# Turning the normalised rows by blocks on VectorE and placing them by transfers, places sent tile by tile, and one shared tile for the ends of W1 and W2

## The reference

```python
x = x + xattn(layernorm(x), ctx, ctx, mask)         # 16 heads, softmax(q k^T / 4) v, then w_o
y = layernorm(x);  idx = top_k(y @ w_router, 128)   # ffn layer, per batch
h = rmsnorm(y[idx], g1); attn = causal_attention(h @ W_qkv.T) @ W_out.T
h2 = rmsnorm(y[idx] + attn, g2)
ff = silu(h2 @ W1.T) * (h2 @ W2.T) @ W3.T           # inner width 682 = 5 x 128 + 42
out = x + y with rows idx of y replaced by y[idx] + attn + ff
```

## Time and profile before

| | us |
|---|---|
| median of 3 runs (lowest, highest) | 889.56 (888.82, 891.79) |
| the profiled execution | 880.62 |
| its span | 878.9 |
| PE busy | 852.3 (97%) |
| ACT busy | 570.7 (65%) |
| DVE busy | 312.4 (36%) |
| POOL busy | 122.7 (14%) |

### The profile page before, as it was taken

One profiled execution on the slowest core, in us unless ns is written; L12 is line 12 of the kernel. 1 busy time (PEld: TensorE's weight loads), 2 busy tenths in 40 slices (PEclk: granted clock), 3 DMA queues, 4 the chain that ended last, 5 costly groups with the idle time before them and its releaser, 6 DMA issues. The chain is left out here.

```text
span 878.9 us, 28281 instructions
## 1 busy us (share of the span) xinstructions
PE 852.3 (97%) x11797; PEld 297.4 (34%) x11802; DVE 312.4 (36%) x915; ACT 570.7 (65%) x648; POOL 122.7 (14%) x174
## 2 busy tenths in 40 slices
PE   7999999999999999999999999999999999999875
PEld 2322232334323433334323333233323342234343
DVE  3122245421552326421453216522274213322442
ACT  3567667676677767676677766777676766776310
POOL 4000102110120101111121101201021101200111
PEclk9999999999999999999999999999999999999999
DMA  5060101120011200211011200112002100010000
GB/s 186 14 234 3 64 17 33 54 76 11 3 37 50 80 8 27 61 32 50 8 39 50 80 8 2 37 50 80 7 5 60 32 3 7 14 49 3 7 25 11
DMA packets 27579, 35.58 MB, mean 40 GB/s; under 512 B 2083, under 2 KB 24142, under 8 KB 27448
## 3 DMA queue, kind: packets, MB, share of 16 engines
q1 hardware_dynamic: 24952, 31.73, 11.3%
q0 software_dynamic: 2496, 1.98, 1.4%
HBM read 27.53 MB, written 8.93 MB: 41 GB/s over the span
## 5 line engine op out<-in xcount | busy, mean ns | idle before, releaser
L524 ACT ACTIVATE probs<-pair_bank 128x1024 f32<-128x1024 f32 x512 | 496.4, 1021 | 222.9 <-ACTq L523 221.7
L494 PE MATMUL pair_bank<-q_sb,k_sb 32*64 32x512 f32 x4096 | 291.2, 612 | 0.4 <-PEq L492 0.3
L513 PE MATMUL o_bank<-probs,va 128*32 128x512 f32 x2048 | 274.7, 604 | 3.0 <-issue 1.5
L513 PEld LDWEIGHTS o_bank<-probs,va 128*32 128x32 f32 x2048 | 41.7, 108 | 208.2 <-issue 113.8
L494 PEld LDWEIGHTS pair_bank<-q_sb,k_sb 32*64 32x64 f32 x4096 | 62.3, 129 | 134.8 <-issue 133.5
L271 PE MATMUL m_bank<-wv_sb,ctx_in 128*32 128x256 f32 x1024 | 62.2, 380 | 0.0
L271 PE MATMUL m_bank<-ctx_in,wk_sb 128*32 128x512 f32 x480 | 61.0, 592 | 0.0
L649 DVE TENSOR_SCALAR va<-m_bank,valid 128x256 f32<-128x256 f32 x64 | 28.1, 479 | 82.8 <-DVEq L646 82.7
L605 DVE STREAM_TRANSPOSE o_blk<-o_bank 128x512 f32<-128x512 f32 x32 | 22.9, 717 | 96.4 <-DVEq L604 96.4
L271 PEld LDWEIGHTS m_bank<-wv_sb,ctx_in 128*32 128x32 f32 x1024 | 33.5, 110 | 35.9 <-issue 21.3
L271 PEld LDWEIGHTS m_bank<-hid_t,w 128*32 128x32 f32 x1392 | 39.4, 110 | 17.2 <-issue 16.3
(11 more groups left out here) (175 smaller groups left out, 627.3 us busy)
## 6 DMA issues: line engine op xcount, KB each, us to landing
ctx_in<-in_ctxT SPq DMA_DIRECT2D x7, 1024.0 KB, 4.9
x_in<-in_x SPq DMA_DIRECT2D x8, 512.0 KB, 3.9
x<-in_x SPq DMA_DIRECT2D x8, 512.0 KB, 4.3
mask_in<-in_mask SPq DMA_DIRECT2D x8, 512.0 KB, 3.9
out_dram<-base SPq DMA_DIRECT2D x8, 512.0 KB, 5.6
ctx_in<-in_ctxT SPq DMA_DIRECT2D x2, 512.0 KB, 6.9
mask_row<-in_mask SPq DMA_DIRECT2D x8, 128.0 KB, 3.9
x_tok<-in_order SPq DMA_DIRECT2D x7, 128.5 KB, 2.0
```

The source lines that it names most:

```text
L494: last = nc.tensor.matmul(pair_bank[pairs[r // 2]][j:j + 64, r % 2], key_tile(b, s, r)[:, j:j + 64], query_tile(b, s, r), start=True, stop ...
L513: last = nc.tensor.matmul(o_bank[32 * r:32 * r + 32], va[b % 2][:, t, HV * h:HV * h + 32], probs[s % 2][:, r], start=(t == 0), stop=(t == ...
L524: nc.scalar.activation(probs[s % 2][:, 2 * e:2 * e + 2, :], pair_bank[p][:], ACT.Exp, scale=HD ** -0.5).then_inc(s_free[p], 1)
```

## The change

Six things are done.

1. From batch 1 on, TensorE no longer turns the normalised rows. VectorE writes them so that 32x32 blocks lie where a block transpose needs them (stage `blocks`) and turns them by two transposes of 128x512 (stage `turn`). Four transfers place the blocks into a DRAM tensor `turned`, and a fifth loads `xn_t` (`put_blocks`). `Q0`, `Q1` become `R0`, `R1` and wait for that load. Batch 0 keeps the old way.
2. For that `x` is loaded with another mapping of rows to partitions, in four transfers (`load_x_for_blocks`).
3. In the loop the stages `stats`, `blocks` and `turn` stand at the end of VectorE's order for batch b+2, around `down`. GpSimd's `var` moves with them. Batch 0 runs them twice: for batch 1, and at its end for batch 2.
4. ScalarE loses the two copies into `xn_t`, TensorE's steps 7 and 8 (in batch 0, 18 and 21) have no third part.
5. Each tile's place is written right behind its own ranking, with a `drain` ahead of it.
6. The last 42 rows of W2 lie in the free columns of W1's sixth tile. So `w1` has two tiles and not three, and VectorE has two small instructions more (`w_rest`, and the product for those 42 rows).

```diff
-           ("P", "K11:0", 4, False), ("P", "K11:1", 5, False), ("F", "spread", 6, False), ("P", "xT0", 7, False), ("P", "xT1", 8, False),
-           ("P", "Q0:0", 9, False), ("P", "Q0:1", 10, False), ("P", "V1", 11, False), ("P", "Q1:0", 12, False), ("P", "Q1:1", 13, False),
+           ("P", "K11:0", 4, False), ("P", "K11:1", 5, False), ("F", "spread", 6, False),
+           ("P", "R0:0", 9, False), ("P", "R0:1", 10, False), ("P", "V1", 11, False), ("P", "R1:0", 12, False), ("P", "R1:1", 13, False),
...
-POOL_ORDER = [("F", "var"), ("P", "var"), ("F", "scatter"), ("F", "rms0"), ("F", "causal"), ("F", "rms1"), ("P", "differ"), ("F", "add")]
+POOL_ORDER = [("F", "var"), ("F", "scatter"), ("F", "rms0"), ("F", "causal"), ("F", "rms1"), ("P", "differ"), ("X", "var"), ("F", "add")]
+POOL_ORDER_0 = [("P", "var"), ("P", "differ"), ("X", "var")]
...
+        def load_x_for_blocks(sp, b):
+            sp.wait_ge(x_free, 1)
+            sp.sem_inc(x_free, -1)
+            for a in range(QT):
+                sp.dma_start(x_in[32 * a:32 * a + 32], io["x"][b, a * P:(a + 1) * P].rearrange("(t i) d -> i t d", i=32)
+                             ).then_inc(x_ready, 16)
+        def put_blocks(sp):
+            sp.wait_ge(blocks_ready, 1)
+            sp.sem_inc(blocks_ready, -1)
+            for a in range(QT):
+                sp.dma_start(turned[:, a * P:(a + 1) * P].rearrange("(c j) k -> j c k", j=32),
+                             blocks_t[32 * a:32 * a + 32].rearrange("j (c k) -> j c k", k=P)).then_inc(blocks_stored, 16)
+            sp.wait_ge(blocks_stored, 16 * QT)
+            sp.sem_inc(blocks_stored, -16 * QT)
+            sp.wait_ge(x_t_free, 1)
+            sp.sem_inc(x_t_free, -1)
+            sp.dma_start(xn_t[:], turned.rearrange("(c p) s -> p c s", p=P)).then_inc(x_t_ready, 16)
...
-                for f in range(3):
+                for f in range(2 if stage == "w1" else 3):
...
+            elif stage == "blocks":
+                dve.wait_ge(rstd_ready, 1)
+                dve.sem_inc(rstd_ready, -1)
+                by_block = xn[:].rearrange("p t d -> p (t d)").rearrange("p (c t j) -> p c t j", t=QT, j=32)
+                for t in range(QT):
+                    nc.vector.tensor_scalar(by_block[:, :, t], x_in[:, t].rearrange("p (c j) -> p c j", j=32), mv[:, t, 0:1],
+                                            rstd[:, t:t + 1], ALU.subtract, ALU.mult)
+                dve.drain().then_inc(x_free, 1)
+            elif stage == "turn":
+                flat = xn[:].rearrange("p t d -> p (t d)")
+                for half in (slice(0, S), slice(S, 2 * S)):
+                    nc.vector.transpose(blocks_t[:, half], flat[:, half])
+                dve.drain().then_inc(blocks_ready, 1)
...
-                if t > 0:
+                if note is put:
+                    dve.drain()
+                    put(t)
+                elif t > 0:
                     note(t - 1)
...
+                if r == 1:
+                    last = nc.vector.tensor_scalar(w_rest[:], bank[i][W2_REST:W2_REST + REST, 2 * P:3 * P], 0.5, None, ALU.mult)
+                last.then_inc(bank_free[i], 1)
...
+                if r == 1:
+                    nc.vector.tensor_tensor(gate[0:REST, FT - 1], w_rest[:], silu2[r][0:REST, 2 * P:3 * P], ALU.mult)
...
                 for b in range(B):
-                    if b + 2 < B:
-                        load_x(sp, b + 2)
+                    if b == 0:
+                        put_blocks(sp)
+                        load_x_for_blocks(sp, 2)
                     if b > 0:
                         load_selected(sp, b - 1)
...
                         load_ctx(sp, b + 2)
+                        put_blocks(sp)
+                    if b + 3 < B:
+                        load_x_for_blocks(sp, b + 3)
```

More of the change, by code:

```diff
@@ L28 @@
 FT = 6
+REST = DFF - (FT - 1) * P
+W2_REST = 64
 BIG = 2.0 ** 30
@@ L188, in program @@
         silu2 = [sb(f"silu2{r}", [P, 3 * P]) for r in range(2)]
+        w_rest = sb("w_rest", [REST, P])
         gate = sb("gate", [P, FT, P])
```

65 lines of the change are left out of this document (41 added, 24 removed), and 13 rows, old and new, of tables (DVE_ORDER, PE_SLOT_0).

## The result

The changed kernel takes 877.92 us (median of 4 runs, 876.13 to 878.86), the kernel before, run beside it, 889.19 us (888.12 to 891.79): a ratio of 0.9867, 95% interval 0.984 to 0.9894, or 11.3 us less. The forecast was 882.5 us and 7.1 us less. The profiled execution after took 877.64 us, which is also the middle of its plain runs; that of before (880.62) is not. By the profiles the two kernels differ by 3.0 us, by the plain runs by 11.3. The reason for this gap turned out to be the cause of the error too.

The account below looks back on a forecast made before the run. TensorE, busy 97% of the span, was taken as the bound. 5.0 + 0.2 + 3.1 - 1.2 = 7.1 us gained gave 873.5 us profiled and 882.5 us as the median of runs, range 877.5 to 888.

Parts of the forecast that it names:

- steps 7 and 8, batches 1 to 6: TensorE steps losing their transposes: the pair takes 4.43 us instead of 5.26, 0.83 per batch, 5.0 us gained.
- steps 18 to 22 of batch 0: Batch 0's emptied steps 18 and 21: only step 18 counted, 0.2 us gained, ends 0 and 0.5.
- step 28, seven batches: w1 with two tiles, 16 products instead of 24: 0.44 us shorter in seven batches, 3.1 us gained.
- step 1 of batch 1 (`norm3` late): VectorE's added work at batch 0's end makes `norm3` late; TensorE waits 1.2 us once, ends 0 and 2.5.
- step 9, six batches: Full step behind the emptied ones: starts with ScalarE's lag already paid, its scores at once, no cost.
- tail: Kernel's end: shorter w1 and VectorE's added `w_rest` meet, 0; ends 0.3 us gained, 0.2 lost.
- VectorE at the other batches' ends: Batches 1 to 5: 5.6 us of work fits 6.11 us idle ahead of `down`'s read-out, about 0.5 spare; cost 0.
- The 74 us: Placing blocks by the strided-copy rule: nearest load taken 19 times, against 28 us of cover; not expected to apply.
- I take the difference as constant: Plain runs' median lies 8.9 us above the profiled execution; gain taken from the median, giving 882.5 us.
- places tile by tile: 0: Chosen rows' places written earlier: 3.4 us of room in batches 1 to 6, extra drains fall into waits, no gain.
- More comes free: Rival: batch 7's stop goes (2.1 us) and batch 0's `norm3` is not late (1.2): 879.2 us, chance 0.13.
- ScalarE's lag: Rival: lag from step 6's scores copy makes step 9 wait 0.35 us more; gain 5.0, 884.6 us, chance 0.15.

Follow-up runs that it names:

- e8: The kernel before, unchanged, run again with a profile on a chip where it is slow: about 890 us, profile 891.9 us.
- e13: Kernel before with only each tile's place written right behind its own ranking, where the kernel before takes about 890 us: 885.5 us, ratio 0.995.
- e5: Changed kernel plus a fifth scatter per batch, of the fourth's rows into a DRAM tensor nothing reads: 881.7 us, 0.9924 of the kernel before.
- e2: Kernel before with only each tile's place written right behind its own ranking, where the kernel before takes about 879.5 us: 880.3 us, ratio 1.0004.
- e11: The same kernel as e2, run again where the kernel before takes about 879.5 us: 879.9 us, ratio 1.0006.
- e6: Changed kernel with batch 2's statistics, blocks and turn done earlier inside batch 0: 876.4 us, 0.9862 of the kernel before.
- e15: e6 with V1 moved to step 9, R0 to steps 10 and 11, V1's read-out ahead of the fourth tile's ranks: 871.5 us, 0.9795 of the kernel before.

## Why the prediction was wrong

*What held.* The free chip is the place of the profile that I worked from. There the spans differ by 877.0 - 870.0 = 7.0 us, against a sum of 7.1. The terms, as measured in that pair:

| term | forecast | measured |
|---|---|---|
| steps 7 and 8, batches 1 to 6 | -5.0 | -4.92 |
| steps 18 to 22 of batch 0 | -0.2 | -0.23 |
| step 28, seven batches | -3.1 | -2.40 |
| step 1 of batch 1 (`norm3` late) | +1.2 | +1.75 |
| step 9, six batches | 0 | +0.37 |
| steps with a stop ("issue") in either kernel | 0 | -1.53 |
| tail | 0 | +0.28 |
| the rest | 0 | -0.32 |

Step 28 gives 0.38 where it gave anything and 0.10 in batch 4. `norm3` was 1.2 us late as said, but the hand-over behind it has two waits, `o_bank` and the products, and the term was read from the second alone. The tail's 0.28 lies past the 0.2 that I gave as an end, but can't be told from chance: from the last scores on, the tail takes 61.3, 59.3 and 63.4 us in three executions of the kernel before. VectorE at the other batches' ends fitted with 0.9 us to spare, where I had 0.5, and the loads never came late: between batches 2 and 3 the four stores start at 319.80, the load of `xn_t` at 324.50, and such a load lands in 3.9 us, 8.6 us in all. The 74 us that I had worked out from the rule on strided copies did not come.

*Where it failed.* Two steps. The first is the sentence "the median of the runs shown is 8.9 us above the profiled one; I take the difference as constant". It is not constant, and it was work for the forecast. In the trace of e8, where the kernel before takes 890 us, 9.5 us are one wait, in step 11 of six batches, and the profile that I worked from does not have it. (The plain runs at 889 left no trace of their own; that they had this wait is concluded from e8, and from the changed kernel's profile of the same set, which has the rest of it.) 1% between a profile and the plain runs of a kernel was a finding to be explained, not an offset; all profiles after it (878.7 to a median of 879.3, 871.9 to 872.5, 891.9 to 890.4, 877.6 to 877.9, and so on) lie within 2.7 us of the median of their runs. The second is "places tile by tile: 0". I priced it by the use of the rows and by the drains, and did not ask what the scatters do to others when they start elsewhere. On a held chip the places are worth 882.5 - 877.9 = 4.6 us in the changed kernel, since all scatters then start earlier, and the read-out stands 0.7 to 0.9 us where it stood 1.5 to 2.0. By the steps 11 of e8 and the changed kernel it is 5.7 us. With 4.6 more the forecast would have been 877.9; that it meets the measured median so well is luck.

By the trace of the kernel before alone the price could not be known: its scatter at 252.08 and read-out at 252.17 (shown with e8) lie side by side without a wait. What it did show is that they lie side by side, in a kernel whose plain runs took 9 us more than the profile.

*The rivals.* "More comes free" (879.2) named the time nearly, but its two parts did not bring it: the stop of the earlier trace rows did go (step 14 of batch 7 is 2.35 us shorter), others of 0.7 us each came in steps 15 and 20, and `norm3` was late. ScalarE's lag did not run on: the scores of step 9 are followed by their values without a wait.

*Is it a port?* A GpSimd scatter and a VectorE instruction could exclude each other at SBUF. The Trainium skill's page "SBUF — State Buffer", section "Who interferes with whom", describes such an exclusion: VectorE and GpSimd share one pair of ports to SBUF, the one that takes it first keeps it for its instruction and the other stands; copies and `tensor_scalar` can be among those that ask for it. The copy that was due 0.64 us after the scatter and stood for a microsecond would fit. The copies that began 0.66 and 1.05 us after a scatter on the same chip do not, nor does ScalarE, which stood as well. The same section says that an instruction with at most one input in SBUF, outside VectorE's modes that use the second port, is not touched. The transposing read of `o_bank` in e13, with no input in SBUF, came 0.74 us late beside a scatter, so something else than this port holds it. The traces thus speak against the port; what is left is the late signal of TensorE, and its cause is open.

*What stays open.* Why the kernels of one set are held and those of another aren't, and what delays TensorE's signal. Why the stops on PE marked "issue" sit where they do: they stand at steps 12 of batch 0, 17 of batch 2 and 14 of batch 7 in three executions of the kernel before on both kinds of chip, and move when the program is changed, even where TensorE's part of it is not (e5 has none in step 15 of batch 7, where the changed kernel has one in both executions). But they are not the same in every execution of a kernel: step 12 of batch 0 takes 2.95 us in one profile of the changed kernel and 4.04 in the other, and step 14 of batch 7 takes 5.26, 4.71 and 2.68 us in e2, e11 and e13, which are one kernel. They are worth some 1 to 3 us from kernel to kernel, so that much of a forecast is luck.

## What to carry to other kernels

Where plain runs and the profile of one kernel differ by more than the runs among themselves, ask first which wait could be there in the one and not in the other, and take a second profile. An indirect DMA that GpSimd issues can be an event for the engines that wait for TensorE, too: price where it starts against each short read-out that TensorE in turn waits for, and keep it over 1.8 us ahead of one or let it start behind it. When an engine starts late beside such an event, look whether the other engines do, and whether its instructions without a wait do, before the engine itself is blamed. Swapping two products in TensorE's table cost nothing, and on a held chip it gave some 4 us (4.0 by steps 9 and 11 of e6 and e15, 4.8 by their medians, which come from two sets), nearly as much as the emptied steps.

## What the runs showed of the hardware that I had not expected

A scatter of 128 rows occupies GpSimd for 0.97 us by the profile, but on a held chip VectorE stood at a wait for TensorE until 0.7 to 1.8 us after the last one's start, and ScalarE until 1.8 us after it in e8. On a free chip the read-outs beside a scatter started on time. A copy that began 0.6 to 0.7 us after a scatter's start took 0.32 to 0.38 us instead of 0.18, on free and held chips alike. Block transposes that write SBUF from SBUF took 0.65 us for 128x512, and writing normalised rows in pieces of 32 elements cost the same 1.38 us for four as whole rows.
